# Attention in a decoder kernel: values and row sums in one run of products, the output half a group later

## The reference

```
x1 = layernorm(x + mixer(x))                      # a gated recurrence, computed as masked products
q, k, v = x1 @ Wq + bq, ctx @ Wk + bk, ctx @ Wv + bv
s  = q_h . k_h / sqrt(8), masked by key           # 16 heads of 8 features
x2 = layernorm(x1 + softmax(s) @ v_h, joined, @ Wo + bo)
out = layernorm(2 * x2 + experts(x2))             # 16 experts and a shared one, top groups and top experts
```

## Time and profile before

| | |
|---|---|
| median of three runs | 603.42 us |
| the profiled execution's own time | 599.92 us |
| its span, first to last instruction | 598.2 us |
| TensorE busy | 545.5 us (91%) |
| VectorE busy | 445.2 us (74%) |
| ScalarE busy | 280.1 us (47%) |
| GpSimd busy | 229.1 us (38%) |
| mean granted clock of TensorE | 0.97 |

### The profile page before, as it was taken

One profiled execution on the slowest core, in us unless ns is written; L12 is line 12 of the kernel. 1 busy time (PEld: TensorE's weight loads), 2 busy tenths in 40 slices (PEclk: granted clock), 3 DMA queues, 4 the chain that ended last, 5 costly groups with the idle time before them and its releaser, 6 DMA issues. The chain is left out here.

```text
span 598.2 us, 17812 instructions
## 1 busy us (share of the span) xinstructions
PE 545.5 (91%) x6344; PEld 452.9 (76%) x6344; DVE 445.2 (74%) x1080; ACT 280.1 (47%) x556; POOL 229.1 (38%) x273
## 2 busy tenths in 40 slices
PE   5769999999999669999999999878999999999994
PEld 5748877787788547878778777767888888888883
DVE  3857877877798487778778787665796887877963
ACT  2358647756675316556556455533323323233220
POOL 2233546534753665244543546713022032131122
PEclk9979999999999958999999999998999999999998
DMA  7124232312332762654654455007246265165160
GB/s 217 38 99 124 76 97 75 122 53 90 102 119 65 200 184 77 185 143 128 173 149 122 136 142 168 7 5 177 65 115 143 63 150 132 60 164 128 38 157 18
DMA packets 55217, 67.42 MB, mean 113 GB/s; under 512 B 6705, under 2 KB 33104, under 8 KB 55152
## 3 DMA queue, kind: packets, MB, share of 16 engines
q1 hardware_dynamic: 52976, 63.58, 39.3%
q0 software_dynamic: 704, 1.92, 1.1%
q10 hardware_dynamic: 1472, 1.05, 0.8%
HBM read 49.26 MB, written 11.21 MB: 101 GB/s over the span
## 5 line engine op out<-in xcount | busy, mean ns | idle before, releaser
L1253 ACT ACTIVATE prob<-bank 128x512 f32<-128x512 f32 x128 | 69.4, 595 | 41.1 <-PE bank L1499 34.8
L2031 PE MATMUL bank<-xT_hl_c,w_up 128*128 128x512 f32 x288 | 85.9, 422 | 2.9 <-ACTq L67 2.9
L1948 ACT ACTIVATE sg<-bank 128x512 f32<-128x512 f32 x72 | 43.1, 598 | 95.2 <-PE bank L2031 89.7
L1349 DVE TENSOR_REDUCE nmax<-bank 128x4 f32<-128x512 f32 x112 | 71.9, 684 | 20.6 <-PE bank L1499 19.3
L2042 PEld LDWEIGHTS bank<-w_down,hid 128*128 128x128 f32 x576 | 73.9, 191 | 10.8 <-DVE hid L1988 3.7
L2042 PE MATMUL bank<-w_down,hid 128*128 128x128 f32 x576 | 76.4, 276 | 2.4 <-DVE res L124 1.5
L1489 PE MATMUL bank<-neg_i,mask 64*128 64x256 bf16 x512 | 52.1, 283 | 12.8 <-DMA q_stack<-q_scratch 4.3
L2031 PEld LDWEIGHTS bank<-xT_hl_c,w_up 128*128 128x128 f32 x288 | 50.2, 194 | 10.0 <-issue 3.1
L1988 DVE TENSOR_TENSOR hid<-gu,share 128x512 f32<-128x512 f32 x64 | 48.9, 763 | 6.0 <-DMA share<-cw_scratch 3.7
L1984 DVE TENSOR_TENSOR gu<-sg,bank_pair 128x512 f32<-128x512 f32 x48 | 32.8, 684 | 19.2 <-ACT sg L1948 13.2
L1747 POOL TENSOR_TENSOR xT_hl_c<-rest,xT_hl_c 128x512 fp32r<-128x512 f32 x7 | 9.0, 1285 | 94.4 <-ACT xT_hl_c L1728 94.4
(11 more groups left out here) (217 smaller groups left out, 1175.2 us busy)
## 6 DMA issues: line engine op xcount, KB each, us to landing
share<-cw_scratch SPq DMA_DIRECT2D x64, 256.0 KB, 5.5
rows<-sum_rows_scratch SPq DMA_DIRECT2D x32, 256.0 KB, 3.5
k_stack<-k_scratch SPq DMA_DIRECT2D x32, 128.0 KB, 2.8
q_stack<-q_scratch SPq DMA_DIRECT2D x32, 128.0 KB, 2.9
prev<-xnext SPq DMA_DIRECT2D x16, 224.0 KB, 2.5
k_scratch<-k_part SPq DMA_DIRECT2D x16, 192.0 KB, 2.4
q_scratch<-q_part SPq DMA_DIRECT2D x16, 192.0 KB, 2.5
x<-xT_in SPq DMA_DIRECT2D x8, 256.0 KB, 8.6
```

Of the source, the lines that this page charges most:

```text
L1253: act.activation(prob[:, b % 2, ORDER[n], :, :], (TT0, TT1)[n % 2][:, :], ACT.Exp, scale=XD ** -0.5)\
L1349: dve.tensor_reduce(nmax[:, b, 4 * u:4 * u + 4], (SS0, SS1)[n % 2][:, :].rearrange("p (i k) -> p i k", i=4), AX_X, ALU.max, negate=True).t ...
L1948: act.activation(sg[:, k, :], GG[k][:, :], ACT.Silu).then_inc(a_s.sem, 1)
L2031: mm = pe.matmul(bank[:, :], w_up[:, which, a, c, :], xT_hl[par][:, v, :], start=(n == 0), stop=(n == 2))
```

## The change

The value matrix `v_d` gets a column of ones for each head in a place that is otherwise zero, so that one product gives a head's values and its row sum. Three of four heads in a row block go into bank U0, the fourth into U1; `weigh` has 8 products per half (h = 0, 1) and no products with ones. The features of Wo and bv are reordered on input so that the four heads interleave. The bias of the values is folded into bo once, before the first group. ScalarE, not VectorE, copies the values into `v_d`. After the last `weigh` of a group ScalarE copies both banks. SyncE stores the sums (two transfers), reloads them as 80 rows and moves the fourth head's rows into place (three transfers). The reciprocal, spread, norm, output and residual of group g now stand in steps (2,0) to (3,1) of group g+1, in bank PF, or PO in the last group; the output of group 7 stands in the experts' stage. The value projection moves to g+1 and in front of step (1,1), the query projection goes to bank PO, and the key projection and x1 transpose of g+3 stand at the end of group g. The lists of all engines are rewritten accordingly; GpSimd's list per group is unchanged.

```diff
+SUMS = 80
...
+def context_out(sp, c, g):
+
+    sp.wait_ge(c.copied.sem, c.copied.at(g, 1))
+    sp.wait_ge(c.d_in.sem, c.d_in.at(g - 1, 1))
+    sp.dma_start(c.of_three, c.raw[0:P:8, 0, :]).then_inc(c.d_out.sem, 16)
+    sp.dma_start(c.of_one, c.raw[1:P:32, 1, :]).then_inc(c.d_out.sem, 16)
+
+
+def context_in(sp, c, g):
+
+    sp.wait_ge(c.d_out.sem, c.d_out.at(g, 1))
+    sp.wait_ge(c.norm.sem, c.norm.at(g - 1, 0))
+    sp.dma_start(c.sums[0:64, :], c.of_three.rearrange("r (b q) -> (r b) q", b=GS)).then_inc(c.d_in.sem, 16)
+    sp.dma_start(c.sums[64:SUMS, :], c.of_one.rearrange("r (b q) -> (r b) q", b=GS)).then_inc(c.d_in.sem, 16)
+    sp.dma_start(c.raw[0:P:4, 0, :], c.raw[0:P:4, 1, :]).then_inc(c.d_move.sem, 16)
+
+
+def invert_sums(dve, c, g):
+
+    dve.wait_ge(c.d_in.sem, c.d_in.at(g, 1))
+    dve.wait_ge(c.p_b.sem, c.p_b.at(g - 1))
+    dve.reciprocal(c.recip[:, :], c.sums[:, :]).then_inc(c.norm.sem, 1)
+
+
+def spread_sums(pe, c, g, bank):
+
+    pe.wait_ge(c.norm.sem, c.norm.at(g, 0))
+    for b in range(GS):
+        mm = pe.matmul(bank[:, b * P:(b + 1) * P], c.pick[0:SUMS, b, :], c.recip[:, :], start=True, stop=True)
+    mm.then_inc(c.p_b.sem, 1)
+
+
+def norm_context(dve, c, g, bank):
+
+    dve.wait_ge(c.p_b.sem, c.p_b.at(g))
+    dve.wait_ge(c.d_move.sem, c.d_move.at(g))
+    dve.tensor_tensor(c.raw[:, 0, :], c.raw[:, 0, :], bank[:, :], ALU.mult).then_inc(c.norm.sem, 1)
+
+
+def context_output(pe, c, t, g, bank):
+
+    pe.wait_ge(c.norm.sem, c.norm.at(g, 1))
+    for b in range(GS):
+        mm = pe.matmul(bank[:, b * P:(b + 1) * P], c.raw[:, 0, b * P:(b + 1) * P], t["w_o"][:, :], start=True, stop=True)
+    mm.then_inc(c.p_o.sem, 1)
...
-    DIAG = P + XD
+    DIAG = P + 1
...
+                context_out(sp, c, g)
+                if left:
+                    context_in(sp, c, g)
...
+            def values(g, par, bank):
+                act.wait_ge(p_v.sem, p_v.at(g))
+                act.wait_ge(p_u.sem, p_u.at(g - 2, GS - 1))
+                for b in range(GS):
+                    dst = v_d[:, par, b, :].rearrange("p (i z) -> p i z", i=UNITS)[:, :, 0:P]\
+                        .rearrange("p i (c e f) -> p i c e f", e=XD, f=4)[:, :, :, :, 0]
+                    act.activation(dst, bank[:, b * P:(b + 1) * P].rearrange("p (c i e) -> p i c e", c=4, i=4), ACT.Copy)\
+                        .then_inc(a_v.sem, 1)
+
             def context(g):
                 act.wait_ge(p_u.sem, p_u.at(g, GS - 1))
                 act.wait_ge(p_o.sem, p_o.at(g - 1))
-                act.activation(ctxT[:, :, :].rearrange("p b t -> p (b t)"), U0[:, :], ACT.Copy).then_inc(a_ctx.sem, 1)
+                for k, bank in enumerate((U0, U1)):
+                    act.activation(c.raw[:, k, :], bank[:, :], ACT.Copy).then_inc(c.copied.sem, 1)
 
             def group(g, par, left):
-                exps(g, 0, 0)
-                if left >= 2:
-                    part_first(act, a, g + 2, par, 1, PF)
-                    x1T_hi(act, a, g + 2, PO)
-                exps(g, 0, 1)
                 if not left:
                     act.wait_ge(e.steps, PREPARED)
                     x2T_hi(act, e, 0, 0)
                 exps(g, 1, 0)
                 if left >= 2:
                     part_second(act, a, g + 2, 1)
-                stack_max(g, par, 1)
                 exps(g, 1, 1)
+                if left:
+                    values(g + 1, 1 - par, PF)
+                else:
+                    logit_tanh(act, e, 0)
                 if left >= 2:
-                    part_first(act, a, g + 2, par, 0, PF)
-                if not left:
-                    logit_tanh(act, e, 0)
+                    part_first(act, a, g + 2, par, 0, PO)
                 exps(g, 2, 0)
+                exps(g, 2, 1)
                 if left >= 2:
                     part_second(act, a, g + 2, 0)
-                exps(g, 2, 1)
                 if left:
                     store_max(g + 1, 1 - par, 0)
+                exps(g, 3, 0)
                 if left >= 3:
                     context_hi(act, a, g + 3, 1 - par)
-                exps(g, 3, 0)
+                exps(g, 3, 1)
                 if left:
                     stack_max(g + 1, 1 - par, 0)
-                exps(g, 3, 1)
-                if not left:
+                    exps(g + 1, 0, 0)
+                    store_max(g + 1, 1 - par, 1)
+                else:
                     copy_weights(act, e, 0, 0)
+                if left >= 3:
+                    part_first(act, a, g + 3, 1 - par, 1, PF)
+                if left:
+                    exps(g + 1, 0, 1)
                 context(g)
-                if left:
-                    store_max(g + 1, 1 - par, 1)
+                if left >= 3:
+                    x1T_hi(act, a, g + 3, PO)
+                if left:
+                    stack_max(g + 1, 1 - par, 1)
...
-
                     dve.wait_ge(e.steps, PREPARED)
                     x2T_lo(dve, e, 0, 0)
-                if not left:
                     expert_scores(dve, e, 0)
                     group_sums(dve, e, 0)
                     rank_groups(dve, e, 0)
                     select_experts(dve, e, 0)
                     share_weights(dve, e, 0)
-                if left:
-                    maxima(g + 1, 3)
+                bank = PF if left else PO
+                if left:
+                    maxima(g + 1, 1)
+                    split_maxima(g + 1, 0)
+                if left >= 2:
+                    part_rest(dve, a, g + 2, 0, PO)
+                if left:
+                    maxima(g + 1, 2, (0, 1))
+                if g:
+                    invert_sums(dve, c, g - 1)
+                if left:
+                    maxima(g + 1, 2, (2, 3))
+                if g:
+                    norm_context(dve, c, g - 1, bank)
+                if left:
+                    maxima(g + 1, 3, (0, 1))
+                if g:
+                    dve.wait_ge(p_o.sem, p_o.at(g - 1))
+                    dve.wait_ge(g_x.sem, g_x.at(g - 1))
+                    residual_sum(dve, g - 1, bank, xb[:, :, :], g_out, v_res, res)
+                if left:
+                    maxima(g + 1, 3, (2, 3))
                     split_maxima(g + 1, 1)
-                invert(g)
                 if left >= 2:
-                    values(g + 2, par)
-                if left:
-                    head(g + 1, 1 - par, left - 1, True)
-                else:
-                    norm(g)
-                    dve.wait_ge(p_o.sem, p_o.at(g))
-                    dve.wait_ge(g_x.sem, g_x.at(g))
-                    residual_dve(dve, g, U1, xb[:, :, :], g_out, v_res, dve_passed, res, stats, mv)
+                    maxima(g + 2, 0, (0, 1))
+                if left >= 3:
+                    part_rest(dve, a, g + 3, 1, PF)
+                if left >= 2:
+                    maxima(g + 2, 0, (2, 3))
+                if left >= 3:
+                    x1T_lo(dve, a, g + 3, PO)
+                if g:
+                    statistics(dve, g - 1, v_res, dve_passed, res, stats, mv)
...
-                if k == (b == GS - 1):
+            def weigh(g, par, b, h):
+
+                if h == 0:
                     pe.wait_ge(a_exp.sem, a_exp.at(g, 4 * b + 3))
-                if k == 0:
-                    pe.wait_ge(v_v.sem, v_v.at(g, b))
+                    pe.wait_ge(a_v.sem, a_v.at(g, GS - 1))
                     if b == 0:
-                        pe.wait_ge(a_ctx.sem, a_ctx.at(g - 1))
-                elif b == 0:
-                    pe.wait_ge(v_res.sem, v_res.at(g - 1, 0))
-                for i in range(4):
+                        pe.wait_ge(c.copied.sem, c.copied.at(g - 1, 1))
+                for i in (2 * h, 2 * h + 1):
                     for u in range(UNITS):
-                        if k:
-                            mm = pe.matmul(U1[32 * u:32 * u + 32, 0:P], ones_s[:, 4 * b + i, :, :].rearrange("p r c -> p (r c)"),
-                                           prob[:, b % 2, u, i, :], start=(b == 0 and i == 0), stop=(b == GS - 1 and i == 3),
-                                           skip_group_check=True)
-                        else:
-                            mm = pe.matmul(U0[32 * u:32 * u + 32, b * P:(b + 1) * P],
-                                           v_d[:, par, b, i * P + 32 * u:i * P + 32 * u + 32],
-                                           prob[:, b % 2, u, i, :], start=(i == 0), stop=(i == 3), skip_group_check=True)
-                if k and b == GS - 1:
-                    mm.then_inc(p_c.sem, 1)
-                elif k or b == GS - 1:
+                        mm = pe.matmul((U0 if i else U1)[32 * u:32 * u + 32, b * P:(b + 1) * P],
+                                       v_d[:, par, b, i * P + 32 * u:i * P + 32 * u + 32], prob[:, b % 2, u, i, :],
+                                       start=i < 2, stop=i in (0, 3), skip_group_check=True)
+                if h:
                     mm.then_inc(p_u.sem, 1)
...
+                bank = PF if left else PO
```

(56 more changed lines are left out.)

186 lines of the change are left out of this document (89 added, 97 removed).

## The result

The changed kernel takes 661.43 us (median of 4 runs, 657.3 to 663.8) against 604.59 us for the kernel before on the same chip: ratio 1.094, 95% interval 1.086 to 1.102. The direction was forecast, the size was not: 632 us was predicted and 643 was the end of the range. The profiled execution has a span of 660.4 us (before 598.2) and a mean granted clock of 0.897.

A forecast was written before the change was run, and what follows sets the result against it. TensorE was read as the bound, with the query transfer chain just hidden behind it and lengthening groups after the change. Terms: 599.92 + 15.0 + 3.7 + 4.0 + 8.5 = 631.1 us; predicted 632, range 608 to 643.

The forecast's parts named there:

- TensorE's saving: Attention groups: eight runs halved to 0.57 us each take out 3.5 us, so TensorE's work falls from 22.1 to 18.5 us.
- The first mark and the first group: Start of the attention groups: first mark at about 251.5 instead of 249.97 us, then groups of 25.1 us.
- the high part of x1: VectorE behind the mark: waits for ScalarE's high part, delaying statistics and maxima; 1.48 us of new wait on TensorE.
- Group: 8.5 + 1.5 + 15.1 = 25.1 us: Attention group: 8.5 from first scores to query projection, 1.5 waiting on VectorE, 15.1 for the chain to the reloaded queries.
- rival 4: Attention and experts' start: the clock falls in new pauses, 1.7 us lost six times, 641 us in all; chance 0.14.
- the splits: VectorE in attention: meeting GpSimd's bias operation, they lose up to 1.1 us a group, counted as nothing in the forecast.
- the query chain: Query projection to first scores, over all engines, store and reload: 14.22 us before, 15.1 forecast, at least 4.2 TensorE idle.
- The weight split: Before the last group: TensorE waits for GpSimd's expert weights, 26.4 us behind the mark against 22.66; +3.7 us.
- End of attention: Last group: GpSimd's bias holds all engines in the stage, about 25.3 us instead of 21.33; +4.0 us.
- Start of the experts: Group 7's output moves here and TensorE pauses until its residual: third gate product at 14.6 instead of 6.78 us; +8.5.
- VectorE's second gated product: Experts' start: its shares are issued behind three new transfers, 1.4 us later; counted at 0.69 us instead of 1.81.

The follow-up runs named there:

- e13: The changed kernel with the edits of e4 and e2 together (earlier maxima reload, idle TensorE products); 640.76 us, ratio 1.065.
- e2: The changed kernel with idle products, used by nothing, put into TensorE's pauses to hold the clock up; 643.03 us, ratio 1.070.
- e5: The changed kernel with e4's earlier reload, and GpSimd's normalisation and bias put behind the third parts of the next stacks; 654.37 us, ratio 1.081.
- e11: e5 with ScalarE's second query part ahead of the exponentials of step (2,1) and VectorE's statistics behind the first split; 634.89 us, ratio 1.055.
- e4: The changed kernel with the reload of the maxima's first half issued before the exponentials of step (3,1), not behind them; 644.53 us, ratio 1.073.
- e3: The changed kernel with GpSimd's normalisation and bias in groups 0 to 4 done on 8 of 128 columns only; 646.61 us, ratio 1.076.
- e6: The changed kernel with expert weights loaded one group earlier, and group 6's statistics and normalisation and group 7's bias add moved into the experts' block; 655.20 us.
- e12: e11 with e6's two moves, the last sums' loads moved ahead, and idle products in two TensorE pauses; 630.04 us, ratio 1.044.

## Why the prediction was wrong

**TensorE's saving, nearly right.** A half run takes 0.57 us (280.10 to 280.67), as taken. 18.5 us of work a group was forecast; 19.2 is what e13 leaves.

**The first mark and the first group, nearly right.** 252.72 for 251.5 and 26.38 for 25.1 us. In this group the chain bounded as described: 15.3 us from the query projection to the first scores, with a pause of 1.78 us ahead of them. VectorE waited 1.08 us for the high part of x1 (257.02), as forecast in kind.

**The step that failed: "Group: 8.5 + 1.5 + 15.1 = 25.1 us", as the length of a group of the kernel after.** The loop that it adds up exists: e13, with the clock held up and the maxima's reload in time, runs it at 9.9 + 15.5 to 16.4 us. In the kernel after it does not set the group from the second group on, because of two things that the sum holds at nothing and one that it leaves out.

First, the clock. The forecast kept it at 1.00; rival 4 had it fall, priced at "six times" 1.7 us, 10 us in all, on the ground that no row of attention showed it. Measured, the same four groups take 118.3 us in the kernel after (252.72 to 371.02) and 104.5 in e2 (249.52 to 354.02), 13.8 us in four groups alone, and e2 is 18 us faster as a whole. So rival 4 had the mechanism, at too low a price.

Second, the splits. The prediction priced them beside GpSimd's bias operation at up to 1.1 us and counted them at "nothing in my forecast, where the reload hides it". They cost 2.5 us, over four operations and not one, and it is the other way round: the late split, with the slow products behind it, hides the query chain. e5 shows both, 0.47 us for 2.79 at the one place and 4.18 us for none at the other. e11 frees both and reaches 24.7 us in spite of a clock of 0.86.

Third, the maxima's own reload was not in the working at all. The change put its issue on ScalarE behind the exponentials of step (3,1), and TensorE waited 16.2 us for it in seven places; before, one wait of 1.3 us near the end.

e4 (reload), e3 (GpSimd) and e2 (clock) each win 15 to 18 us, and two of them together 21. The reading that fits is one loop, cut at different places: at half clock the maxima leave later, their reload lands later, TensorE pauses again, and the clock falls again. No run isolates that feedback, so this reading is argued, not shown.

**The weight split, too long.** +3.7 forecast, +1.5 measured: it ended at 426.12, at mark + 24.2 instead of 26.4. Loads and split took 17.5 us as forecast (17.6); they began at mark + 6.7 and not 8.8. TensorE did wait for the split, 3.30 us.

**End of attention, +4.0 forecast, +8.4 measured.** The mechanism is right: GpSimd's bias ends at 454.24 and the stage with it. (The terms that the prediction names add up to 24.9 us, not to its 25.3.) But this stretch ran at 0.61. Without the wait for the weights and with the bias moved on (e6) it takes 23.1 us at 0.82.

**Start of the experts, +8.5 forecast, +10.9 measured.** The order is the forecast's. VectorE's second gated product waits 2.88 us for its shares, behind the three new transfers, runs at 464.30 and takes 0.69 us as counted (GpSimd's operation beside it ended at 463.77). The reciprocal stands behind it, and TensorE waits 4.8 us for that, then runs at 0.60 over this stretch (0.75 was taken from the earlier trace rows):

```profile
465.91 2.08 PE L1118 MATMUL bank<-recip,pick_s 80*128 80x128 f32 x8 [4.83 <-DVE recip L1111]
468.77 2.07 PE L1133 MATMUL bank<-w_o,ctx_raw 128*128 128x128 f32 x8 [0.78 <-DVE ctx_raw L1126]
```

**What stays open.** e12 is 28 us above the kernel before (630.04 less 602.39), 29.9 between the two profiles. Its four groups take 95.3 us where the kernel before took 90.0: +5.3. From there to the last group's start it is +7.9, to the first product of the experts +2.7, to the third gate product +12.0, and behind it +2.6. So the start of the experts is the largest piece. What holds the two groups before the last was not tested, and the output of group 7 put back into attention was not tried.

## What to carry to other kernels

Work taken off the bounding engine turns into pauses when a chain or another engine stands just behind, and pauses of 2 to 3 us can cost more in clock than they last: price a pause with the half-speed work behind it (some 10 us of it behind the 2.79 us here), and the lateness that this passes on. When an operation moves, lay the two timelines of VectorE and GpSimd over each other at its new place, operation by operation and in every group, the last ones too, and do the same for every transfer that is issued behind it on its queue. A cure that leaves the time as it was, or makes it worse, may still have hit its cause: compare stretch by stretch, and look in the trace for what is late next.

## What the runs showed of the hardware that was not expected

**Small VectorE operations wait for the end of GpSimd's instruction.** Operations of 0.19 us on 128x32 values took 0.45, 1.22, 0.52 and 1.08 us, each ending 0.05 us behind GpSimd's. In e4 it is the same in another group, GpSimd's bias, mask copy and third part ending at 313.14, 313.70 and 314.81:

```profile
312.00 1.20 DVE L1470 TENSOR_TENSOR nrest<-nmax,npart 128x32 f32<-128x32 f32 x1
313.22 0.52 DVE L1472 SCALAR_TENSOR_TENSOR npart<-nrest 128x32 bf16<-128x32 f32 x1
313.77 1.08 DVE L1474 SCALAR_TENSOR_TENSOR npart<-nrest,npart 128x32 bf16<-128x32 f32 x1
```

An operation that reads a bank beside it was not lengthened: the rest at 290.90 took 0.74 us beside a mask copy, 0.75 with GpSimd idle (in e5 at 313.98). The Trainium skill (SBUF — State Buffer, SBUF: two separate sides) calls the ports shared by these engines an exclusive lock, held for the whole instruction; the trace agrees, to 0.05 us.

**The clock can fall at short pauses.** Behind a pause of 2.79 us TensorE ran at the 1.2 GHz level for some 10 us; with 36 idle products a group, 2.4 us of them, it stayed at 1.00 from the second group on (e2, e13). In the kernel before, with no pause over 1.3 us in the groups, it never fell there. The length of a pause alone does not decide it: in e13 the products behind one of 2.75 us (273.87) ran at full speed.
